# Experts of a mixture in a four-layer kernel: 64-row products of two experts each, image by image, with the halves added by a product

## The reference, cut

```python
            shared = jnp.zeros_like(h)
            for s in range(shared_w.shape[0]):
                shared = shared + _gelu(_c1(feats, shared_w[s], shared_b[s])) / shared_w.shape[0]
...
            vals, idx = jax.lax.top_k(scores, TOP_K)
            wts = jax.nn.softmax(vals / TEMPERATURE, axis=1)
            gate_w = jnp.zeros((B, NUM_EXPERTS), x.dtype).at[jnp.arange(B)[:, None], idx].add(wts)
            out = shared
            for e in range(NUM_EXPERTS):
                out = out + _gelu(_c1(feats, expert_w[e], expert_b[e])) * gate_w[:, e][:, None, None, None]
            return out + residual
```

## Time and profile before

| | us |
|---|---|
| median of 3 runs | 7600.77 |
| lowest, highest | 7596.58, 7612.95 |
| the profiled execution | 7609.55 |
| its span in the trace | 7607.1 |

### The profile page before, as it was taken

One profiled execution on the slowest core, in us unless ns is written; L12 is line 12 of the kernel. 1 busy time (PEld: TensorE's weight loads), 2 busy tenths in 40 slices (PEclk: granted clock), 3 DMA queues, 4 the chain that ended last, 5 costly groups with the idle time before them and its releaser, 6 DMA issues. The chain is left out here.

```text
span 7607.1 us, 120115 instructions
## 1 busy us (share of the span) xinstructions
PE 6646.3 (87%) x37246; PEld 3510.5 (46%) x37246; DVE 5727.4 (75%) x5704; ACT 3966.8 (52%) x6794; POOL 3507.3 (46%) x2382
## 2 busy tenths in 40 slices
PE   8968699999966399787999999999989999999970
PEld 7852233333245144673222222222257777777760
DVE  4653677777712287115999999999979999999975
ACT  4424466666611376104666666666555555555532
POOL 0100122222201200003777777777768888888860
PEclk9989799999977699667999999999989999999995
DMA  2253233433356423532000000000000000000016
GB/s 70 71 176 117 71 99 100 101 99 100 93 126 194 185 90 105 132 72 38 19 18 18 19 19 18 18 18 18 9 17 11 9 10 9 10 10 10 8 37 192
DMA packets 618033, 481.73 MB, mean 63 GB/s; under 512 B 248797, under 2 KB 549123, under 8 KB 609435
## 3 DMA queue, kind: packets, MB, share of 16 engines
q1 hardware_dynamic: 617819, 479.02, 23.2%
HBM read 304.91 MB, written 171.32 MB: 63 GB/s over the span
## 5 line engine op out<-in xcount | busy, mean ns | idle before, releaser
L2556 DVE TENSOR_TENSOR_SCAN spa_hs<-spa_p_d,spa_hs,spa_bx 128x483 f32<-128x483 f32 x1168 | 1476.2, 1404 | 0.0
L2282 POOL TENSOR_TENSOR spa_hc<-spa_hs,spa_cr 128x966 f32<-128x966 f32 x592 | 1224.4, 2068 | 426.8 <-DVE spa_hs L2556 410.5
L2687 POOL TENSOR_TENSOR spe_hc<-spe_hs,spe_cu 128x1024 f32<-128x1024 f32 x520 | 1216.1, 2359 | 274.6 <-DVE spe_hs L2884 274.6
L2884 DVE TENSOR_TENSOR_SCAN spe_hs<-spe_p_d,spe_bx 128x1024 f32<-128x1024 f32 x520 | 1161.0, 2274 | 6.5 <-ACT spe_p_d L2833 5.9
L1065 DVE TENSOR_REDUCE attention_nm<-attention_p_s 128x2 f32<-128x640 f32 x1024 | 789.1, 812 | 259.2 <-PE attention_p_s L922 258.1
L2761 PE MATMUL spe_p_y<-spe_idt,spe_hc 128*128 128x128 f32 x8320 | 973.3, 275 | 0.0
L2761 PEld LDWEIGHTS spe_p_y<-spe_idt,spe_hc 128*128 128x128 f32 x8320 | 951.7, 192 | 0.0
L1023 ACT ACTIVATE attention_pr<-attention_p_t 128x512 f32<-128x512 f32 x1280 | 710.6, 598 | 418.6 <-PE attention_p_t L945 287.5
L2467 ACT ACTIVATE spa_p_d<-spa_p_d,spa_av 128x483 f32<-128x483 f32 x1184 | 705.1, 634 | 409.6 <-PE spa_p_d L2339 407.6
L2833 ACT ACTIVATE spe_p_d<-spe_p_d 128x896 f32<-128x896 f32 x520 | 445.5, 899 | 795.4 <-PE spe_p_d L2746 795.2
L2542 DVE TENSOR_TENSOR spa_bx<-spa_br,spa_p_u 128x952 f32<-128x952 f32 x592 | 780.0, 1318 | 33.5 <-PE spa_p_u L2352 33.4
(11 more groups left out here) (423 smaller groups left out, 10396.9 us busy)
## 6 DMA issues: line engine op xcount, KB each, us to landing
attention_qs<-scratch_qp SPq DMA_DIRECT2D x768, 64.0 KB, 2.8
attention_rc<-scratch_den SPq DMA_DIRECT2D x128, 256.0 KB
scratch_qp<-patch_parts SPq DMA_DIRECT2D x64, 384.0 KB, 2.3
spa_xt<-scratch_x SPq DMA_DIRECT2D x148, 121.5 KB, 2.6
front_xs<-in_x_dram SPq DMA_DIRECT2D x64, 256.0 KB, 3.0
scratch_xf<-front_out SPq DMA_DIRECT2D x128, 128.0 KB, 2.5
patch_x<-scratch_xf SPq DMA_DIRECT2D x8, 2048.0 KB, 18.8
attention_xs<-in_x_dram SPq DMA_DIRECT2D x128, 128.0 KB, 4.7
```

The costliest lines, as they stand in the source:

```text
L2282: nc.gpsimd.tensor_tensor(hc[:, k % 8:k % 8 + 2, :], hs[:, k:k + 2, :], cr2[:, s % 2, :].unsqueeze(1).broadcast_to([128, 2, NA]), ALU.mult ...
L2556: nc.vector.tensor_tensor_scan(hs[:, k, v], p_d[k % 4][:, v], bx[:, k, v], 0.0 if start else hs[:, k, NA - 1:NA], ALU.mult, ALU.add).then_ ...
L2687: nc.gpsimd.tensor_tensor(hc[:, k, :, d, :].rearrange("p s d t -> p d s t"), hs[:, k % 2, d, :, :], rows, ALU.mult)\
L2884: nc.vector.tensor_tensor_scan(hs[:, k % 2, d].rearrange("p d s t -> p (d s t)"), p_d[h][:, :], bx[:, k % 2, d].rearrange("p d s t -> p (d ...
```

## The change

It rewrites `experts` and the layout of the shared weights.

- A chunk is again 512 pixels of an image pair, but each product contracts the 64 channels of one image and gives two experts at once, 128 output rows: `p_x[k][p]` for image p of the pair, k = 0 and 2 with two chosen experts each, k = 1 with both shared ones. That makes six products of 64 rows. DVE, ACT and POOL therefore work on tiles whose two halves are two experts of one image.
- The shared experts' Gelu goes to SBUF (`gs`); POOL multiplies it by a tile of one half (`share`) into `us`. DVE's first addition is k = 0 times its gates plus `us`, into `acc`; the second adds k = 2. There are two of each for a chunk, one for each image.
- Two more products on PE, one for each image, add the upper and the lower half of `acc` (`fold` is two identities, one above the other); the results are the two halves of `p_o`. DVE adds `hr` to it (`finish`), one chunk later.
- The engines' loops go through `stream`, four chunks a turn, and waits count chunks. `stream` and `after` are moved up in the file, unchanged. The loaded features `fs` have four buffers, `gs`, `us`, `acc` and `os` two.
- The matrices of the chosen experts have no zero blocks. DVE and POOL each make half of the multiplications `pk`; DVE makes all sums, eight over all partitions. 13 loads, four of which gather every second expert's gate or choice. The stage has 20 semaphores, before 16.

```diff
+def after(eng, sem, n):
+    if not (isinstance(n, int) and n <= 0):
+        eng.wait_ge(sem, n)
...
-def experts(nc, hr, feats, sel, wts, we, be, ws, bs, out1):
-    NF = HW // 512
+def experts(nc, hr, feats, sel, wts, we, be, ws, bs, ident, out1):
+    NCH, UX, NP = 2 * (HW // 512), 4, NX // 2
...
+        hot2 = st.sb("hot2", [128, B * TOP // 2, NE])
+        pk = st.sb("pk", [128, 2, C, NE])
+        pb = st.sb("pb", [128, B * TOP // 2, NE])
+        wsh = st.sb("wsh", [128, 2 * C])
+        bsh = st.sb("bsh", [128, 1])
+        wx = st.sb("wx", [128, 2, TOP // 2, 2 * C])
+        bx = st.sb("bx", [128, B, TOP // 2])
+        gx = st.sb("gx", [128, B, TOP // 2])
+        idt = st.sb("idt", [128, 128])
+        fold = st.sb("fold", [128, C])
+        share = st.sb("share", [128, 512])
+        fs = st.sb("fs", [128, UX, 512])
+        gs = st.sb("gs", [128, 2, 2, 512])
+        us = st.sb("us", [128, 2, 2, 512])
+        acc = st.sb("acc", [128, 2, 2, 512])
         os = st.sb("os", [128, 2, 512])
-        p_x = [st.ps(f"p_x{k}", [128, 512]) for k in range(NX)]
-        loaded, zeroed, step, w_ready = st.sem("loaded"), st.sem("zeroed"), st.sem("step"), st.sem("w_ready")
-        f_in, x_done, x_ready = st.sem2("f_in"), st.sem("x_done"), st.sem("x_ready")
-        summed = [st.sem(f"summed{k}") for k in range(NX)]
-        stored = st.sem2("stored")
-        N = NF // 2
+        p_x = [[st.ps(f"p_x{k}{p}", [128, 512]) for p in range(2)] for k in range(NP)]
+        p_o = [st.ps(f"p_o{s}", [128, 512]) for s in range(2)]
...
+            for p in range(2):
                 for a in range(2):
-                    b = 2 * q + a
+                    b = 2 * a + p
+                    sp.dma_start(hot[64 * p:64 * p + 64, a].rearrange("p k e -> p (k e)"),
+                                 sel.rearrange("b k e -> b (k e)")[b:b + 1, :].broadcast_to([64, TOP * NE])).then_inc(loaded, 16)
+            with nc.allow_non_contiguous_dma(reason="every other expert's gate"):
+                for q in range(2):
                     r = slice(64 * q, 64 * q + 64)
-                    sp.dma_start(hot[r, a].rearrange("p k e -> p (k e)"),
-                                 sel.rearrange("b k e -> b (k e)")[b:b + 1, :].broadcast_to([64, TOP * NE])).then_inc(loaded, 16)
-                    sp.dma_start(gx[r, a, NSH:NX], wts[b:b + 1, :].broadcast_to([64, TOP])).then_inc(loaded, 16)
-            def load(n, s):
-                sp.dma_start(fs[:, s, :], fv[:, bass.ds(n * 512, 512)]).then_inc(f_in[s], 16)
-
-            def store(a, j, s):
-
-                sp.wait_ge(summed[NX - 1], a * N * 2 + 2 * j + s + 1)
-                sp.dma_start(ov[:, a, bass.ds((2 * j + s) * 512, 512)], os[:, s, :]).then_inc(stored[s], 16)
-
+                    sp.dma_start(hot2[r], sel.rearrange("b (k q) e -> q (b k) e", q=2)[q:q + 1].broadcast_to([64, B * TOP // 2, NE]))\
+                        .then_inc(loaded, 16)
+                    sp.dma_start(gx[r].rearrange("p b k -> p (b k)"),
+                                 wts.rearrange("b (k q) -> q (b k)", q=2)[q:q + 1].broadcast_to([64, B * TOP // 2])).then_inc(loaded, 16)
+            def load(c, s, r):
+                after(sp, x_done, 2 * NP * (c - 3))
+                sp.dma_start(fs[:, s, :], feats[:, s % 2, columns(s, r)]).then_inc(f_in[s], 16)
+            def store(c, s, r):
+                sp.wait_ge(out_ready, c + 1)
+                sp.dma_start(ov[:, s % 2, columns(s, r)], os[:, s % 2, :]).then_inc(stored[s % 2], 16)
+            stream(sp, NCH, UX, 2 * UX, 4, (0, load), (4, store))
...
+        @block.tensor
+        def _(pe):
+            def spread(c, s, r):
+                pe.wait_ge(f_in[s], 16 * r + 16)
+                for k, (free, n) in enumerate(((first_added, 2), (shared_active, 2), (last_added, 2))):
+                    for p in range(2):
+                        after(pe, free, n * c + (p - 1))
+                        rows = slice(64 * p, 64 * p + 64)
+                        w = wsh[rows, :] if k == 1 else wx[rows, s % 2, k // 2, :]
+                        nc.tensor.matmul(p_x[k][p][:, :], w, fs[rows, s, :], start=True, stop=True).then_inc(x_done, 1)
+            def add_halves(c, s, r):
+                after(pe, out_ready, c - 1)
+                for p in range(2):
+                    pe.wait_ge(last_added, 2 * c + (p + 1))
+                    mm = nc.tensor.matmul(p_o[s % 2][64 * p:64 * p + 64, :], fold[:, :], acc[:, s % 2, p, :], start=True, stop=True)
+                mm.then_inc(folded, 1)
+            pe.wait_ge(loaded, 16 * 13)
+            pe.wait_ge(w_ready, 2 * TOP + 2)
+            stream(pe, NCH, UX, UX, 1, (0, spread), (1, add_halves))
...
+            def activate(c, s, r):
+                b = lambda p: 2 * (s % 2) + p
+                for k in range(NP):
+                    for p in range(2):
+                        act.wait_ge(x_done, 2 * NP * c + (2 * k + p + 1))
+                        if k == 1:
+                            after(act, shared_scaled, 2 * c + (p - 3))
+                            nc.scalar.activation(gs[:, s % 2, p, :], p_x[k][p][:, :], ACT.Gelu, bias=bsh[:, 0:1]).then_inc(shared_active, 1)
+                        else:
+                            nc.scalar.activation(p_x[k][p][:, :], p_x[k][p][:, :], ACT.Gelu, bias=bx[:, b(p), k // 2:k // 2 + 1])\
+                                .then_inc(first_active if k == 0 else last_active, 1)
+            act.wait_ge(w_ready, 2 * TOP + 2)
+            stream(act, NCH, UX, UX, 0, (0, activate))
...
+            def choose(a, k, t):
+                nc.vector.tensor_reduce(wx[:, a, k // 2, C * (k % 2):C * (k % 2) + C], pk[:, t], AX.X, ALU.add).then_inc(w_ready, 1)
+            dve.wait_ge(loaded, 16 * 13)
+            nc.vector.tensor_tensor(fold[:, :], idt[:, 0:C], idt[:, C:2 * C], ALU.add).then_inc(w_ready, 1)
+            link(nc.vector.tensor_tensor(pb[:, :, :], hot2[:, :, :], bes[:, :].unsqueeze(1).broadcast_to([128, B * TOP // 2, NE]), ALU.mult))
+            nc.vector.tensor_reduce(bx[:, :, :].rearrange("p b k -> p (b k)"), pb[:, :, :], AX.X, ALU.add).then_inc(w_ready, 1)
+            for i in range(TOP):
+                for t in range(2):
+                    a, k = (2 * i + t) // TOP, (2 * i + t) % TOP
+                    if t == 0:
+                        if i:
+                            dve.wait_ge(w_ready, 2 * i + 1)
+                        link(nc.vector.tensor_tensor(pk[:, 0], wes[:, :, :], hot[:, a, k, :].unsqueeze(1).broadcast_to([128, C, NE]), ALU.mult))
+                    else:
+                        dve.wait_ge(halved, i + 1)
+                    choose(a, k, t)
+            def add(c, s, r):
+                t, b = s % 2, lambda p: 2 * (s % 2) + p
+                for p in range(2):
+                    dve.wait_ge(first_active, 2 * c + (p + 1))
+                    dve.wait_ge(shared_scaled, 2 * c + (p + 1))
+                    after(dve, folded, c - 1)
+                    nc.vector.scalar_tensor_tensor(acc[:, t, p, :], p_x[0][p][:, :], gx[:, b(p), 0:1], us[:, t, p, :], ALU.mult,
+                                                   ALU.add).then_inc(first_added, 1)
+                for p in range(2):
+                    dve.wait_ge(last_active, 2 * c + (p + 1))
+                    dve.wait_ge(first_added, 2 * c + (p + 1))
+                    nc.vector.scalar_tensor_tensor(acc[:, t, p, :], p_x[2][p][:, :], gx[:, b(p), 1:2], acc[:, t, p, :], ALU.mult,
+                                                   ALU.add).then_inc(last_added, 1)
+            def finish(c, s, r):
+                dve.wait_ge(folded, c + 1)
+                after(dve, stored[s % 2], 16 * (r * 2 + s // 2))
+                nc.vector.tensor_tensor(os[:, s % 2, :], p_o[s % 2][:, :], hr[:, s % 2, columns(s, r)], ALU.add).then_inc(out_ready, 1)
+            stream(dve, NCH, UX, UX, 1, (0, add), (1, finish))
+        @block.gpsimd
+        def _(pool):
+            def scale(c, s, r):
+                for p in range(2):
+                    pool.wait_ge(shared_active, 2 * c + (p + 1))
+                    after(pool, first_added, 2 * c + (p - 3))
+                    nc.gpsimd.tensor_tensor(us[:, s % 2, p, :], gs[:, s % 2, p, :], share[:, :], ALU.mult).then_inc(shared_scaled, 1)
+            nc.gpsimd.memset(share[:, :], 1.0 / NSH).then_inc(filled, 1)
+            pool.wait_ge(loaded, 16 * 13)
+            pool.wait_ge(filled, 1)
+            for i in range(TOP):
+                a, k = (2 * i + 1) // TOP, (2 * i + 1) % TOP
+                if i:
+                    pool.wait_ge(w_ready, 2 * i + 2)
+                nc.gpsimd.tensor_tensor(pk[:, 1], wes[:, :, :], hot[:, a, k, :].unsqueeze(1).broadcast_to([128, C, NE]), ALU.mult)\
+                    .then_inc(halved, 1)
+            stream(pool, NCH, UX, UX, 0, (0, scale))
...
-    k["sw"] = np.stack([twice(w.T) for w in p("shared_w")], 1)
-    k["sb"] = dup(p("shared_b").T)
+    k["sw"] = dup(p("shared_w").transpose(2, 0, 1).reshape(C, 2 * C))
```

(1 more changed line is left out.)

127 lines of the change are left out of this document (26 added, 101 removed).

## The result

The changed kernel took 7702.6 us (7695.0 to 7707.7, four runs) against 7606.9 us for the kernel before (four runs): a ratio of 1.0125, interval 1.011 to 1.014. It is slower, as forecast, but by 96 us and not by 44, and outside the stated range (7612 to 7692). Six of the 58 us between 7645 and 7702.6 are the base: the forecast started from 7600.8. The two profiled executions have spans of 7607.1 and 7701.3 us, so 94.2 us are to be found.

The account below looks back on a forecast made before the run. It took PE to bound the experts' loop before, and a ring of waits through DVE, PE, ACT and POOL after; +57.2 us for the loop and -13 for the weights, against 7600.77, gave 7645 us, range 7612 to 7692.

Parts of the forecast that it names:

- The ring: Experts' loop: waits from DVE's first addition through PE, ACT, POOL back to it set 6.04 us a chunk, against 5.17.
- The first chunk: Start of the experts' loop: 8.8 us to the end of the second image's first addition.
- The 64-row products do run side by side: PE in the experts' loop: six products cost about 2.6 us; the rival that they do not (4%) gave 7699 us.
- the clock stayed at 0.99: PE in the experts' loop: forecast 1.00; the rival that its clock falls (14%) gave 7703 us, or 7674 for half the chunks.
- The weights: Making the chosen experts' weights before the loop: 30.8 us before, a gain of 13 us taken.
- I take -13 us, as the collision row is the nearest: Weights: a first-stage row where DVE's addition beside POOL took 1.05 us, not 0.61; 0.44 more in each of four collisions.
- my 17.5 and 21.7: Weights' length in us: 17.5 with four collisions (gain 13.3), 21.7 if DVE and POOL exclude each other (gain 9.1).
- the sum without overlap: Weights if DVE and POOL exclude each other: 6.9 + 3 x 4.93 = 21.7 us.
- 17 to 18 us from last load to first product: Sign named in advance for the weights, to be seen in the changed kernel's trace if the forecast held.
- I count 0, with ends -0.5 and +2: Loads at the experts' stage's start: 13 in place of 14, four gathering 64-byte or 4-byte pieces, counted at 0 us.
- +57.2 - 13 = +44.2 us: Whole kernel: the loop's +57.2 us (392.8 against 335.6) and the weights' -13 us.
- the two rivals that they name: Experts' loop: the ring does not bind (7%, 7539 us); the ring is shorter, 5.3 to 5.5 us (9%, 7604 us).

Follow-up runs that it names:

- Experiments 3: Changed kernel with the shared experts' product and activation first in each chunk: 7576.0 us, 0.9993 of the kernel before; experts' stage 332 us against 432.
- 4: Changed kernel without POOL's scaling (factor 1/2 in the halves' sum, gates doubled once): 7580.4 us, 0.9999 of the kernel before; experts' stage 318 us.
- 8: Changed kernel with every POOL scaling done twice, first into an unread tile: experts' stage 637.7 us against 431.8; no total time given.

## Why the prediction was right and wrong

**The ring: right.** One period of the changed kernel's loop, word for word (the terms follow from the starts):

```profile
2864.40 0.75 DVE L1976 SCALAR_TENSOR_TENSOR experts_acc<-experts_p_x,experts_gx,experts_us 128x512 f32<-128x512 f32 x1 [0.47 <-POOL experts_us L1999]
...
2865.20 0.18 PEld L1911 LDWEIGHTS experts_p_x<-experts_fs,experts_wx 64*128 64x128 f32 x1 [0.93 <-DVE experts_acc L1976]
...
2866.36 0.66 ACT L1936 ACTIVATE experts_p_x<-experts_p_x,experts_bx 128x512 f32<-128x512 f32 x1 [0.56 <-PE experts_p_x L1911]
...
2866.95 1.26 ACT L1934 ACTIVATE experts_gs<-experts_p_x,experts_bsh 128x512 f32<-128x512 f32 x2
...
2867.78 2.49 POOL L1999 TENSOR_TENSOR experts_us<-experts_gs,experts_share 128x512 f32<-128x512 f32 x2 [3.48 <-ACT experts_gs L1934]
...
2870.36 0.75 DVE L1976 SCALAR_TENSOR_TENSOR experts_acc<-experts_p_x,experts_gx,experts_us 128x512 f32<-128x512 f32 x1 [0.47 <-POOL experts_us L1999]
```

| term | forecast | measured |
|---|---|---|
| DVE to PE | 0.06 | 2865.20 - 2865.15 = 0.05 |
| PE to the activation's start | 1.24 | 1.16 |
| ACT, second to third | 0.58 | 0.59 |
| ACT's third, to POOL | 0.69 + 0.08 | 0.83 |
| POOL, two products | 2.54 | 2.49 |
| POOL to DVE, DVE's sum | 0.10 + 0.75 | 0.84 |
| period | 6.04 | 5.96 here, 5.97 in the mean |

The loop was 4.6 us shorter than forecast, of which 4.2 are the 63 periods (376.3 us in place of 380.5). The first chunk took 8.7 us (8.8 forecast). Experiments 3, 4 and 8 show each side of it: take the scaling out of the round and the loop falls by 100 us or more, double it and the period grows by 2.7 us at full clock. The 64-row products do run side by side, and the clock stayed at 0.99.

**The weights: right in kind, off by 2.4 us.** The step that was off is "I take -13 us, as the collision row is the nearest". That row had DVE's addition begun while a second POOL instruction was about to start; in four true collisions the whole instruction was waited for. The 20.2 us lay between my 17.5 and 21.7: the first pair took 6.3 us where 6.9 stood in the sum without overlap, and the rounds behind it 4.6 to 4.7 where 4.93 stood. The "17 to 18 us from last load to first product" that would have shown the forecast right didn't come.

**The start loads: mis-sized.** "I count 0, with ends -0.5 and +2": +9.8 us. The row I leaned on the earlier trace rows is a load of whole rows, 1 KB in 2.3 us; the new one is cut into 4-byte pieces, and no row of the trace had such. So the nearest row was the wrong kind of row. Neither the size in KB nor the number of pieces gives the time alone: the two loads of hot2 (32 KB each) have as many pieces, 512 each, of 64 bytes, and landed after 3.7 us once the gates' loads were gone. Why the 4-byte pieces take longer stays open.

**The step that failed: what the sum left out, 43.8 us.** "+57.2 - 13 = +44.2 us" has terms of the experts' stage alone, so it puts the change of all other stages at nothing, and gives no reason. They did change, since their loops moved in the engines' programs. That term, +6.7 and +37.1, is the larger part of the miss, and alone takes 7645 to 7689, near the range's end; with the loads' 9.8 it is out of it. Why these stages took longer is shown as far as the place in the program goes; the piece's length and the store behind it are argued. Nothing in the profile of before pointed at it but part 3 of the page, whose instruction queues I had passed over; the 15 packets in 1600 us of loop said that PE's loop fitted, not how nearly. That the result was slower at all doesn't hang on this term: the stage of the experts alone is 52 us longer.

A slip that changes nothing here: the chances put 0.18 on same and faster, where the two rivals that they name have 0.16 together.

The remainder, +2.0 ahead of the stage and -3.4 behind it, is as large as the difference between two runs of one kernel.
